# Attention and mixture-of-experts block on one core: another split of PSUM between maxima and scores, and row maxima transposed by VectorE

## What is computed

```python
def _L0_attn_ref(x, Wq, bq, Wk, bk, Wv, bv, Wo, bo):      # 16 heads of 16
    ...
    scores = jnp.einsum('bqhd,bkhd->bhqk', Q, K) * scale
    scores = scores + _alibi_bias(S, H, x.dtype)[None]
    attn = jax.nn.softmax(scores, axis=-1)
    out = jnp.einsum('bhqk,bkhd->bqhd', attn, V).reshape(B, S, D)
    return out @ Wo + bo
def _L0_ffn_ref(x, Wg, W1, W2, W3, Ws1, Ws2, Ws3):        # 8 experts, top 2, plus a shared one
    ...
    h = jax.nn.silu(jnp.einsum('tc,ech->eth', xf, W1)) * jnp.einsum('tc,ech->eth', xf, W2)
    y = jnp.einsum('eth,ehc,te->tc', h, W3, w)
    hs = jax.nn.silu(xf @ Ws1) * (xf @ Ws2)
    y = y + (hs @ Ws3).reshape(b, t, c)
x = L0_attn_x
xn = _layernorm(x, axis=-1)
x = x + _L0_attn_ref(xn, ...) + _L0_ffn_ref(xn, ...)
```

## Time and profile before

| | |
|---|---|
| median of 3 runs | 2506.57 us (2504.11 to 2506.87) |
| the profiled execution, its own time | 2505.09 us |
| its span, first to last instruction | 2503.3 us |
| TensorE busy | 2456.3 us, 98% |
| TensorE weight loads | 1649.2 us, 66% |
| VectorE busy | 2052.1 us, 82% |
| ScalarE busy | 1658.8 us, 66% |
| GpSimd busy | 843.7 us, 34% |
| mean granted TensorE clock | 0.993 |

### The profile page before, as it was taken

The page is one execution under the profiler, slowest core; times in us unless marked ns, Lnnn a source line. Parts: engine busy times, 40 slices in busy tenths (PEclk is TensorE's granted clock), DMA queues, the critical chain, the costliest instruction groups (busy, mean ns, idle before and its releaser), DMA issues.

```text
span 2503.3 us, 51165 instructions
## 1 busy us (share of the span) xinstructions
PE 2456.3 (98%) x20186; PEld 1649.2 (66%) x20186; DVE 2052.1 (82%) x3521; ACT 1658.8 (66%) x2314; POOL 843.7 (34%) x929
## 2 busy tenths in 40 slices
PE   6999999999999999999999998999999999999999
PEld 5775444444444444444444445999999988888887
DVE  7977999999999999999999993777777765554444
ACT  3445777787788888888888887777777753333222
POOL 3332332332101115555411112333333334444444
PEclk9998999999999999999999999999999999999999
DMA  8985443544222235555422233777777743444332
GB/s 285 339 298 177 153 142 122 161 145 140 76 68 78 80 85 160 157 154 154 147 76 76 75 118 105 237 237 239 239 241 241 242 152 102 121 117 116 102 102 85
DMA packets 213599, 384.41 MB, mean 154 GB/s; under 512 B 45444, under 2 KB 134724, under 8 KB 203988
## 3 DMA queue, kind: packets, MB, share of 16 engines
q1 hardware_dynamic: 175088, 218.25, 28.3%
q0 software_dynamic: 37184, 162.09, 20.4%
q10 hardware_dynamic: 1088, 0.79, 0.1%
HBM read 249.10 MB, written 141.49 MB: 156 GB/s over the span
## 4 chain that ended last, share of the span: by engine, by line
PE 93%; ACT 3%; issue 1%; DVE 1%; DMA 1%; SPq 0%; POOL 0%; ACTq 0%; DVEq 0%; POOLq 0%
PE ps L490 91%; PE ps L503 3%; ACT pta L799 1%; ACT ptb L799 0%; ACT mT L788 0%; DMA Wvst<-in_Wg 0%; ACT qkH L775 0%; SPq L1389 0%; DVE qkL L934 0%; DMA xr<-Xn 0%; DVE xn L918 0%; DVE XL L926 0%; DMA OPS<-Alid 0%; POOL vs L1183 0%; DVE VB L1083 0%
## 5 line engine op out<-in xcount | busy, mean ns | idle before, releaser
L944 DVE TENSOR_REDUCE mx<-ps 128x1 f32<-128x512 f32 x2048 | 1262.0, 680 | 34.6 <-PE ps L490 19.0
L490 PE MATMUL ps<-OPS 52*128 52x512 f32 (+1 forms) x4096 | 821.2, 452 | 9.5 <-ACT pta L799 1.8
L490 PEld LDWEIGHTS ps<-OPS 54*128 54x128 f32 (+1 forms) x4096 | 426.4, 186 | 507.9 <-issue 203.9
L799 ACT ACTIVATE pta<-ps 128x1024 f32<-128x1024 f32 x512 | 510.4, 1023 | 150.8 <-PE ps L490 143.4
L799 ACT ACTIVATE ptb<-ps 128x1024 f32<-128x1024 f32 x512 | 510.9, 1024 | 116.5 <-PE ps L490 116.2
L490 PE MATMUL ps<-OPS,WB 128*128 128x256 f32 (+1 forms) x2268 | 363.5, 312 | 2.9 <-DVE VB L1083 1.6
L490 PEld LDWEIGHTS ps<-OPS,WB 128*128 128x128 f32 x2268 | 310.5, 180 | 32.3 <-issue 3.3
L490 PE MATMUL ps<-pta,VB 128*32 128x352 f32 (+1 forms) x4096 | 302.6, 390 | 0.0
L490 PE MATMUL ps<-ptb,VB 128*32 128x352 f32 (+1 forms) x4096 | 301.4, 389 | 0.0
L1227 POOL TENSOR_TENSOR accs<-accs,asum 128x512 f32<-128x512 f32 x64 | 81.7, 1277 | 586.7 <-DMA asum<-Sd 561.6
L490 PE MATMUL ps<-OPS,WB0c 128*128 128x256 f32 (+3 forms) x1440 | 257.9, 330 | 3.8 <-issue 2.8
(11 more groups left out here) (155 smaller groups left out, 2755.0 us busy)
## 6 DMA issues: line engine op xcount, KB each, us to landing
OPS<-QKh SPq DMA_DIRECT2D x512, 64.0 KB
Xs<-zero POOLq DMA_DIRECT2D x71, 256.0 KB, 3.3
xr<-Xs SPq DMA_DIRECT2D x71, 256.0 KB, 5.3
Ys<-VB SPq DMA_DIRECT2D x71, 256.0 KB, 5.0
QKh<-qkH SPq DMA_DIRECT2D x16, 1024.0 KB, 7.2
QKl<-qkL SPq DMA_DIRECT2D x16, 1024.0 KB, 8.9
OPS<-QKl SPq DMA_DIRECT2D x256, 64.0 KB
asum<-Sd SPq DMA_DIRECT2D x64, 256.0 KB
```

The source lines that it names most:

```text
L490: return self.e.matmul(o, l, r, start=start, stop=stop)
L799: self.e.activation(pt(n), ps[:, b:b + 2, :], ACT.Exp).then_inc(sem["exp"], 1)
L944: e.reduce_max(mx[:, k2, hh, i, half:half + 1], ps[:, bank, :], AX.X).then_inc(sem["mxred"], 1)
```

## The change

The maxima get four banks (4 to 7), the scores three single banks (0 to 2), the accumulator bank 3. Each exponential covers one bank, that is one head, key block and half; the two halves of one head follow each other now, and the maxima's units run in the same pattern on the other head. ScalarE issues 32 exponentials of 512 columns for each pair instead of 16 of 1024. The turn of mneg goes from TensorE (and the copy from ScalarE) to one VectorE transpose in 32x32 blocks, which leaves the 32 rows of mneg in four groups of partitions of mT, 32 queries each. SP therefore writes them into QO with eight DMAs, each of 16 rows by 32 numbers. max_rows stands at the first P of key block 4 instead of the second, and AHEAD is 56. Counts of smm and exp double.

```diff
-AHEAD = 52
+AHEAD = 56
...
-            if n >= 32 and not rows0:
-                self.max_rows(0, 7)
+            if n >= 36 and not rows0:
+                self.max_rows(0)
...
-                        self.scores(r, kc + i // 4, i % 2, i // 2 % 2)
+                        self.scores(r, kc + i // 4, i // 2 % 2, i % 2)
...
-                    if v == 1 and kc == 4 and r + 1 < NPAIR:
+                    if v == 0 and kc == 4 and r + 1 < NPAIR:
...
-        return 5 + self.turns.index((what, i)) % 3
+        return 4 + self.turns.index((what, i)) % 4
...
-        mT = sbuf(ctx, "mT", [32, 2, P], F32R)
+        mT = sbuf(ctx, "mT", [P, 2, 32])
...
             def scores(self, r, kc, hh, half):
-                k, h0, n = r % 4, 64 * hh, 16 * r + 2 * kc + half
-                bank = 2 * (n % 2) + hh
+                k, h0, n = r % 4, 64 * hh, 32 * r + 4 * kc + 2 * hh + half
                 self.w.wait_ge(f"op{k}", 256 * (r // 4 + 1))
-                self.w.wait_ge(f"mx{r % 2}", 32 * (r // 2 + 1))
+                self.w.wait_ge(f"mx{r % 2}", 128 * (r // 2 + 1))
...
-                self.w.wait_ge("exp", n - 1)
-                if kc == 5 and half == 0 and hh == 1:
-                    self.w.wait_ge("mrev", min(r + 2, NPAIR))
-                q = self.mm(ps[:, bank, :], KO[h0:h0 + KEXP, k, kc * P:(kc + 1) * P],
-                            QO[h0:h0 + KEXP, k, half * GT:(half + 1) * GT], True, True)
-                if hh == 1:
-                    q.then_inc(sem["smm"], 1)
+                self.w.wait_ge("exp", n - 2)
+                self.mm(ps[:, n % 3, :], KO[h0:h0 + KEXP, k, kc * P:(kc + 1) * P],
+                        QO[h0:h0 + KEXP, k, half * GT:(half + 1) * GT], True, True).then_inc(sem["smm"], 1)
...
-                self.e.activation(pt(n), ps[:, b:b + 2, :], ACT.Exp).then_inc(sem["exp"], 1)
+                self.e.activation(pt(m)[:, half * GT:(half + 1) * GT], ps[:, n % 3, :], ACT.Exp).then_inc(sem["exp"], 1)
...
+            def max_rows(self, r):
+
+                self.w.wait_ge("mnl", r + 1)
+                self.w.wait_ge(f"mx{r % 2}", 128 * (r // 2))
+                self.e.transpose(mT[:, r % 2, :], mneg[:, r % 2, :, :, :].rearrange("p h l i -> p (h l i)")
+                                 ).then_inc(sem["mtr"], 1)
...
-            def max_rows(self, r, bank=None):
-                self.w.wait_ge("mrev", r + 1)
+            def max_rows(self, r):
+                self.w.wait_ge("mtr", r + 1)
                 for hh in range(2):
-                    self.e.dma_start(QO[64 * hh + 52:64 * hh + 54, r % 4, :].bitcast(F32).rearrange("l (i n) -> l i n", n=P),
-                                     mT[16 * hh:16 * hh + 16, r % 2, :].bitcast(F32)).then_inc(sem[f"mx{r % 2}"], 16)
+                    for b in range(4):
+                        c0 = 32 * b + 16 * hh
+                        self.e.dma_start(QO[64 * hh + 52:64 * hh + 54, r % 4, :].bitcast(F32)
+                                         .rearrange("l (i b n) -> l b i n", i=8, b=4)[:, b, :, :],
+                                         mT[c0:c0 + 16, r % 2, :]).then_inc(sem[f"mx{r % 2}"], 16)
```

More of the change, by code:

```diff
@@ L52 @@
     "vst asd sdw asb ox0 ox1 zero wd xg0 xg1 sc0 sc1 wb0 wb1 wb2 xs0 xs1 xs2 xs3 yr0 yr1 xr0 xr1 oro ga0 ga1 ga2 ga3 res "
-    "xt qkmm vmm mxmm mrt smm pv rtmm sct gmm up down sdn "
-    "wsplh woh xh qkh vev mrev exp acc1 rte wsh sch sg hh yev och "
-    "wspll bq wol st ag ve norm xl qkl mxred m16 rcp rt rtm rtd rtw rts rtp rtc wslv scl hf hl ocl s1 gf fin "
+    "xt qkmm vmm mxmm smm pv rtmm sct gmm up down sdn "
+    "wsplh woh xh qkh vev exp acc1 rte wsh sch sg hh yev och "
+    "wspll bq wol st ag ve norm xl qkl mxred m16 mtr rcp rt rtm rtd rtw rts rtp rtc wslv scl hf hl ocl s1 gf fin "
     "nhalf rstd lgc vad pad vcp ones zmem mng mnh mnl nrm wslp xb ya"
@@ L274, in max_unit, with max_rows @@
     def max_unit(self, n, bank=None): pass
-    def max_rows(self, r, bank=None): pass
+    def max_rows(self, r): pass
     def load_v(self, b, f): pass
@@ L545, in ring_bank @@
                 at = ring.turns.index((what, i))
-                if at >= 3:
-                    was, j = ring.turns[at - 3]
+                if at >= 4:
+                    was, j = ring.turns[at - 4]
                     if was == "max":
@@ L782, in project_v @@
                 self.e.copy(vs[:, k, j, :], ps[:, bank, 0:D + NE]).then_inc(sem["vev"], 1)
-            def max_rows(self, r, bank=None):
-                bank = 1 if bank is None else bank
-                self.w.wait_ge(f"mx{r % 2}", 32 * (r // 2))
-                self.w.wait_ge("mrt", r + 1)
-                self.e.copy(mT[:, r % 2, :], ps[0:32, bank, 0:P]).then_inc(sem["mrev"], 1)
-            def scores(self, r, kc, hh, half):
-                if hh == 0:
-                    return
-                n = 16 * r + 2 * kc + half
-                b = 2 * (n % 2)
-                if n % NPT >= NPT // 2:
+            def scores(self, r, kc, hh, half):
+                m, n = 16 * r + 2 * kc + hh, 32 * r + 4 * kc + 2 * hh + half
+                if m % NPT >= NPT // 2:
                     projections_over(self.w)
-                self.w.wait_ge("pv", n // 2 - 3)
+                self.w.wait_ge("pv", m // 2 - 3)
                 self.w.wait_ge("smm", n + 1)
-                self.e.activation(pt(n), ps[:, b:b + 2, :], ACT.Exp).then_inc(sem["exp"], 1)
+                self.e.activation(pt(m)[:, half * GT:(half + 1) * GT], ps[:, n % 3, :], ACT.Exp).then_inc(sem["exp"], 1)
             def values(self, r, kc, v):
@@ L805, in values @@
                     self.w.wait_ge("pv", 8 * (r + 1))
-                    self.e.copy(accs[:, r % 2, :], ps[:, 4, :]).then_inc(sem["acc1"], 1)
+                    self.e.copy(accs[:, r % 2, :], ps[:, 3, :]).then_inc(sem["acc1"], 1)
             def route(self, i):
@@ L1215, in max_unit @@
                     e.tensor_scalar(m16[:, k2, :, :], m16[:, k2, :, :], -1.0, None, ALU.mult).then_inc(sem["mng"], 1)
-                    self.w.wait_ge("mrt", r - 1)
+                    self.w.wait_ge("mtr", r - 1)
                     self.w.wait_ge("mng", r + 1)
```

46 lines of the change are left out of this document (17 added, 29 removed).

## The result

| | before | after |
|---|---|---|
| median | 2505.34 us (2502.41 to 2506.87, 4 runs) | 2553.49 us (2543.74 to 2563.07, 4 runs) |
| ratio of the two | | 1.0193, 95% interval 1.0146 to 1.0241 |
| the profiled execution, its own time | 2505.09 us | 2563.07 us |
| its span | 2503.3 us | 2560.9 us |
| mean granted TensorE clock | 0.993 | 0.973 |

The change costs 48 us, 1.9%; the whole interval of the ratio lies above 1. The prediction was 2555 us, and its range of 2498 to 2605 holds the result. The profiled execution is the slowest of the four, 9.6 us above their median. The other three read clocks of 0.982, 0.975 and 0.979 at 2543.74, 2559.73 and 2547.25 us, so the executions differ as their clocks do. Before, the spread was 4.5 us. That is the first sign that more than the length of SP's path is at work.

What follows compares the result with a forecast made beforehand. VectorE was taken to bound the kernel before, and SP's path with eight mT issues to bound the changed one. 2505.1 + 53 for longer pairs - 2 for 56 ahead = 2556, written as 2555 us; range 2498 to 2605.

Steps and rivals of the forecast that it cites:

- What the trace was to show: Expected signs: mT issues near 0.7 apart, first-score wait 1 to 2 us, maxima 0.60 apart, VectorE's share some 92%.
- Bounds before: Of 20.19 us a pair, VectorE's floor is 19.5, TensorE's 19.2; SP's path has 1.9 to about 3.5 to spare.
- The term that decides: eight issues: SP's mT DMAs: 0.73 us from start to start, so the eighth starts 5.1 us after the first.
- rival A: VectorE stays the bound at 19.7 us a pair if a small issue is well under 0.56; 2478 us, chance 0.17.
- Landing: End of SP's path: mT rows land 2.0 us after the last issue starts, 2.4 when scattering, plus 0.1 to restart.
- The sum by stages: Longer pairs: 21 early ones +6 us, ten +11, sixteen scattering +24, eleven of the last +12; together +53.
- I add nothing: TensorE clock: most gaps taken as too short, so 0; +1.5 us a pair for 16 pairs kept for the range.
- Rival D: TensorE's gap drops the clock in many pairs: the forecast and 25 to 40 us more, 2590 us, chance 0.12.
- VectorE's floor: VectorE's own time per pair: 19.5 us plus 0.16 for the transpose, 19.7 us.
- Fourth bank, exponentials, transposes: VectorE no longer starves for maxima; single-bank exponentials stay hidden on ScalarE, 0.1 us a pair; transpose 0.16 us on VectorE.
- rival C: Three score banks starve ScalarE or TensorE, 0.15 us at each of 8 hand-overs a pair; 2530 us, chance 0.08.
- 56 ahead: Four more maxima before the first score, +2.4 us once; with gains elsewhere -2 together; mneg causes no wait.

Runs made afterwards that it cites:

- e2_before_swap: The kernel before with load_pair's sixteen DMAs issued ahead of the sums of the pair before, nothing else; 2510.19 us, ratio to before 1.0022.
- e14_before_56: The kernel before with AHEAD = 56 instead of 52 and nothing else; 2497.48 us, ratio to before 0.9966.
- e7_dum_ahead: The kernel before with six more small DMAs to a scratch area on SP, directly ahead of its two mT DMAs; 2565.05 us, ratio to before 1.0230.
- e1_swap: The changed kernel with the sixteen loads of a later pair issued ahead of the sums on SP, nothing else; 2464.87 us, ratio to before 0.9835.
- e12_swap_ring3: The changed kernel with the loads ahead of the sums and three banks for the maxima instead of four; 2486.91 us, ratio to before 0.9928.
- e13_dvet_swap_56: The kernel before with VectorE's transpose, its eight DMAs, loads ahead of the sums and AHEAD = 56; 2488.48 us, ratio to before 0.9930.
- e4: The kernel before with VectorE's transpose, its eight DMAs and loads ahead of the sums, AHEAD still 52; 2526.04 us, ratio to before 1.0080.

## Why the prediction was right, and where its terms were not

**What the trace was to show.** The wait at the first score, the maxima 0.60 apart and a shorter wait of SP for accs (347.1 us for 499.3) are there; the eight issues are 0.67 apart, not 0.7 or more, and VectorE's share is 97% (195.60 of 201.02) where nothing scatters and 85% (317.13 of 374.62) where rows are scattered, not 92% throughout.

**Bounds before.** Right. e2_before_swap leaves the period at 20.18, so SP's path did not bind; e14_before_56 leaves it near there too.

**The term that decides: eight issues.** Right in kind, and a little small in size. Over all 512 of them:

```profile
L1381 SPq DMA_DIRECT2D OPS<-mT x512: 596/611/1181, 183.7 to 1563.5; - x171
```

The median is 0.611 us, against 0.654 for the two of before. From start to start it is (5.30 - 0.61) / 7 = 0.67 for my 0.73, which came from a pair's first two issues (the first is the longest of a row). Seven of them are 4.7 us, not 5.1. The break-even I had put at 0.56, rival A's way in, was closer than the forecast of 0.73 made it look. The prediction's range had a case for 0.65, near the truth. Over 61 pairs the missing 0.4 us is 25 us: with this term mended alone, the sum would have been 2531. In pairs 24 to 33, where nothing scatters, the path had more to spare than I took: in the kernel before, the next first score stands 4.60 us (mean) behind the end of the second mT issue, of which the landing needs 1.14. That leaves 3.5 for the 4.0 us of new issues, and sq comes 0.37 earlier: nothing was lost there.

**Landing.** I had taken 2.0 from the start of the last issue with a quiet DMA, and 2.4 with scattering. With the restart, 2.1 and 2.5. It was 1.14 + 0.61 = 1.75, and 2.71 + 0.6 = 3.3 in the scattering pairs. Sd, the row I leaned on the earlier trace rows, told the quiet landing within 0.4, but not what the scattering does to an mT DMA.

**The sum by stages.** Pairs 24 to 33: +11 forecast, -1.0 measured. Pairs 34 to 49: +24, measured +51.6. Pairs 50 to 61: +12, measured +13.7. Early pairs: +6 forecast (21 x 0.25 is 5.3, and the path with a quiet landing had been 21.3, not the 21.2 taken here); 402.91 - 209.46 = 193.45 for the nine first ones is 7 less than the 411.76 - 211.32 = 200.44 of before, the fifteen next +3.4. Sum +57.6 with the -1.9 ahead of the first score and the -1.2 behind pair 61, in the profiled execution; +48 between the medians. So the headline fell within 2 us of the median **because two errors cancel**: the early pairs and the ten from 24 on were some 20 us cheaper, the scattering ones 27 dearer. The mechanism was right; that the number is so near is luck. What failed is the step "I add nothing" for the clock, and beside it the landing of 2.4 in the scattering pairs. Of the 1.7 us by which a scattering pair exceeds its 21.7, 1.4 is the late sq, which is the clock's doing by the reading above, and 0.8 the landing; the shorter issues and loads give back 0.5. Against pairs 24 to 33 of the same trace a scattering pair is 3.31 us longer, and the two have equal parts in it: 7.08 - 5.53 = 1.55 is sq, 2.71 - 1.14 = 1.57 the landing. Rival D had the mechanism and a price of 1.5 a pair, near what happened, but it was added to a forecast that was too dear elsewhere.

The rule of the Trainium skill's page "DMA: Bandwidth & Descriptors" ("Anatomy of one DMA"), by which many descriptors can be emitted before it shows, is stated there for DMAs that GpSimd issues. The prediction held it against DMAs of SP, of which that section says nothing, so it was no support for rival A. What six separate DMAs cost in SP's queue is shown by e7_dum_ahead, 4.0 us.

**VectorE's floor.** The forecast said 19.7; e1_swap runs at 19.54 to 19.55 with VectorE 99.8% busy. The transpose is 0.20 us long. In the pair at 1377.95 it starts at 1389.51, with the maxima resuming at 1389.63, so it holds the stream up 0.12 for my 0.16. Rival A's 2478, which is this floor, is thus 2465 as measured.

**Fourth bank, exponentials, transposes.** Right. The fourth bank takes the 0.44 of starving away (e12_swap_ring3), exponentials of one bank cost nothing to be seen (e13_dvet_swap_56 beside e12_swap_ring3; 0.60 us long each, where I had said 0.58), and rival C's ring of three never bound.

**56 ahead.** The +2.4 is confirmed by 2.5 and 1.9 us at the first score, and the turn's wait of 2.03 is gone. But "no wait" for mneg was all I said of its use. It is what keeps the negation ahead of the product on POOL, worth 37 us in e1_swap and 38 in the step from e4 to e13, 31 to 32 of each in the scattering pairs. In the changed kernel it is worth nothing that can be told, and why the kernel before gains 7 us by it stays open.

**The better version.** The change with the loads ahead of the sums (e1_swap) takes 2464.87 us, 1.65% under the kernel before and 3.5% under the change. The change was not wrong, but incomplete: it moved 4.0 us of issues onto a path that had 1.9 to 3.5 to spare, and the sixteen loads that stand in its way can go out ahead of a wait.

## What to carry to other kernels

Splitting a small DMA into four is paid in issues on its queue, not in bytes. Add them up, from start to start, to the path of whoever waits for the last one, and first move ahead of it what stands in the same queue but is wanted later. Where one step makes a tight queue longer, follow also what comes behind it: here sums, reciprocals and a product on POOL, ahead of which stood the next pair's maxima. And where the path would open gaps on TensorE, price the clock through the path: ask whether a slower start of a stage delays the very transfer that ends it.

## What the hardware showed that I had not expected

A small SBUF to SBUF DMA lands, with the waiting matmul started, 1.14 us after SP's issue ends in pairs 24 to 33 (1.13 to 1.15 in all ten), and 2.71 as a mean, up to 3.66, in pairs 34 to 49, in which POOL's indirect DMAs run. SP's issues of the same form took 0.67 us from start to start, with the first of a row slower (0.72 to the second one) than the later ones (0.65). The granted clock fell after an idle 1.66 us and stood after an idle 1.81 and an idle 2.21; what decides between them I have not settled. Nor is it shown how much of the scattering pairs' loss would stay at a steady clock, since no run here holds the clock and keeps the gaps.
